# A recurrent block on one core: order of the decayed scores and of the 2:4 selection, and a first round with halves of products between the levels

## The chip, the cores and the metric

The kernel runs on one core of one Trainium2 chip. The metric is the device time of one execution in microseconds (us). TensorE is called PE here, VectorE DVE, ScalarE ACT, GpSimd POOL and SyncE SP. "L1275" is line 1275 of the kernel before.

## What is computed

Two blocks follow one another on 2048 tokens of 256 channels (two sequences of 1024). Each is a recurrent mixer, gated by a feed-forward branch, and added to its input.

```python
xn = layernorm(x)
s  = L0_attn(xn)      # five token-shift mixes, r/k/v/g projections, decayed outer-product recurrence
                      # (4 heads of 64), norm per head, times silu gate, output projection
g  = silu(L0_ffn(xn)) # h = silu(x@w_gate) * (x@w_up), 1024 wide;
                      # of each 4 neighbours the 2 largest |h| are kept (2:4); h @ w_down
x  = x + s * g
xn = layernorm(x)
s  = L1_attn(xn)      # state space: 8 heads, chunks of 32, scores C B^T times exp(cs_i - cs_j)
g  = silu(L1_ffn(xn)) # gated feed-forward, 1024 wide, not sparse
x  = x + s * g
```

## The kernel before

The tokens are cut into 8 tiles of 256. The kernel runs nine rounds. Round 1 does the first block of tile 0 alone. Each of the seven rounds of the loop does the first block of tile n (called `a`) and the second block of tile n-1 (called `b`), interleaved by hand. The last round does the second block of tile 7 alone. `one(a, b)` is written once for each engine and holds the order of the steps by hand for three cases: `a and b`, `a` alone (the first round), `b` alone (the last round). Every engine works through its list strictly in order, so a step that waits holds all that stands behind it on its engine.

PSUM has eight banks. Each product has a bank and a turn in it. `FILLS` says which for the loop, `FIRST_FILLS` for the first round. PE may open a bank for a product when the previous product of that bank has been freed by its reader (`open_bank`); the readers wait until it is filled (`wait_filled`).

Steps that matter here, with the lines of their instructions:

- The feed-forward branch of block one makes its hidden units in four pairs: `p0` to `p3`, each with a gate product (`p3g`) and an up product (`p3u`), eight 128x256 matmuls each (`project_p`, matmuls at L1275). ACT makes the tanh (`ffn_tanh`, L500), DVE two products (`hidden_p`, L799 and L803), ACT the absolute values (`ffn_abs`, L507). DVE compares the four neighbours (`compare`, L913), counts (`sparse_count`, L924 to L931) and sets the smaller ones to zero (`sparse_select(0)` for units of p0 and p1, `sparse_select(1)` for p2 and p3, L941). PE multiplies by the down weights (`down_0`, in the first round `down_part`, L1311) after both selections.
- The recurrence of block one runs through seven levels. PE makes the products of a level (`level`, L1364, the last at L1403), DVE multiplies k and r by decays and takes the products (`level_step`, three instructions, L868, L869, L877), and PE may start the next level then. `own_products` (L1384, banks `D0` and `D1`) makes the diagonal, which `own_keys` (L897) takes. After the last level come `last_update` (L868, L869), `keys_turned` (L1596), `chunk_states` (L1610), `states_0` (L992), `outputs` (L1420 to L1431), `centred` (L1006 to L1014), `variances`, the root on POOL, `out_normed` (L1025), `out_turned` (L1324), `out_gated` (L1035) and `out_0` (L1275).
- The state-space part of block two: POOL masks the sums, ACT takes sixteen exponentials (`L_exps(0)` and `L_exps(1)`, eight of 128x128 each, L546), PE makes the scores in four banks (`sc0`, `sc2` by `scores(0)`; `sc1`, `sc3` by `scores(1)`; L1459), and DVE multiplies them (`decayed_scores`, L1096). `sc0` and `sc1` need `L_exps(0)`, `sc2` and `sc3` need `L_exps(1)`. Then `states_1` (L1101, L1104) on DVE; `within` (L1474) on PE waits for all four, and `across` (L1485) for `states_1`. DVE gates the result (`gated_1`, L1114), which frees the banks `ys0` and `ys1` that the products `n1g` and `n1u` of the second feed-forward branch open next.

Of the kernel before, what the change touches and what calls it, by code (L numbers as in the profile page):

```python
# [20 lines left out]
ALU = mybir.AluOpType  # L21
# [54 lines left out]
               ["mix_k", "L1", "kv", "yT"],  # L76
               ["mix_r", "r", "D0", "Y0", "s0"],
               ["a", "mix_v", "v", "D1", "Y1"],
               ["p0g", "w0", "p2g", "g"], ["p0u", "w1", "p2u", "F0"], ["p1g", "mix_g0", "p3g"], ["p1u", "mix_g1", "p3u"]]
FIRST = {n: (b, i + 1) for b, names in enumerate(FIRST_FILLS) for i, n in enumerate(names)}  # L80
# [32 lines left out]
def build_block(nc, A):  # L113
    with ExitStack() as ctx:
# [96 lines left out]
        lev_pair = psum[:, BANK["L0"]:BANK["L0"] + 2, :]  # L211
        own_pair = psum[:, BANK["D0"]:BANK["D0"] + 2, :]

# [277 lines left out]
        def _(act):  # L491
# [44 lines left out]
            def one(a, b):  # L536
# [112 lines left out]
                if a and b:  # L649
# [28 lines left out]
                    end_exp()  # L678
                    L_exps(0)
                    L_exps(1)  # L680
                    ffn_tanh(a, "p3", th[1], th_ready, "p1")
                    copy(a, y[:, :, :], "Y0", NQ)
# [11 lines left out]
                elif a:  # L694
# [12 lines left out]
                    ffn_tanh(a, "p3", th[1], th_ready, "p1")  # L707
                    ffn_abs(a, 2)
                    others()
                    copy(a, k0n[:, :, :], "k0T", NQ)  # L710
                    ffn_abs(a, 3)
                    gate_tanh()
                    copy(a, y[:, :, :], "Y0", NQ)
# [36 lines left out]
        def _(dve):  # L750
# [139 lines left out]
            def own_keys(t):  # L890

                dve.wait_ge(lev_ready, t.count(6, 1))
                dve.sem_inc(passed, 1)
                for e in range(2):
                    wait_filled(dve, t, f"D{e}")
                    dve.sem_inc(passed, 1)
                    free(d.copy_predicated(own[:, e, :, :].rearrange("p g x -> p (g x)"), same[:, 256 * e:256 * e + 256],  # L897
                                           own_pair[:, e, 0:256]), t, f"D{e}")

# [58 lines left out]
            def one(a, b):  # L958
# [131 lines left out]

                def decayed_scores(part):
                    for n in (part, 2 + part):
                        dve.wait_ge(L_exp, b.count(NQ, n // 2 + 1))
                        wait_filled(dve, b, f"sc{n}")
                        w = flat(cs_row)[:, n * 512:(n + 1) * 512]
                        free(d.tensor_tensor(w, w, ps(b, f"sc{n}")[:, :], ALU.mult), b, f"sc{n}")  # L1096

# [30 lines left out]
                if a and b:  # L1128
# [37 lines left out]
                    B_decayed()  # L1166
                    sparse_select(0)
                    decayed_scores(0)
                    hidden_p(a, 3)
                    decayed_scores(1)  # L1170
                    states_1()
                    compare(1)
                    sparse_count()
                    gated_1()
                    sparse_select(1)
# [14 lines left out]
                elif a:  # L1190
# [18 lines left out]
                    level_step(a, 1)  # L1209
                    sparse_sums()  # L1210
                    sparse_rest()
                    level_step(a, 2)
                    mix_g_scaled(a)
                    mix_add(a, "g")
                    level_step(a, 3)
                    hidden_p(a, 2)
                    level_step(a, 4)
                    level_step(a, 5)
                    last_update(a)
                    hidden_p(a, 3)  # L1220
                    sparse_select(0)
                    compare(1)
                    states_0()
                    sparse_count()
                    sparse_select(1)
                    centred()
                    gate_0()
                    variances()
                    out_normed()
                    next_normed()  # L1230
                    out_gated()
# [4 lines left out]
                else:  # L1236
# [7 lines left out]
                    B_decayed()  # L1244
                    decayed_scores(0)
                    decayed_scores(1)
                    hidden_n(b, 2)
# [10 lines left out]
        def _(pe):  # L1258
# [34 lines left out]
            def project_p(t, n, suffix):  # L1293
                hidden_pair(t, f"p{n}{suffix}", {"g": "f_gate", "u": "f_up"}[suffix], n, lambda h: xnT[:, h, 1:T + 1])

            def ffn_p(t, n):
                project_p(t, n, "g")
                project_p(t, n, "u")
# [10 lines left out]
            def down_part(t, q, first, end):  # L1309
                for m in range(first, end):  # L1310
                    ins = t_.matmul(ps(t, "F0")[:, q * C:(q + 1) * C], hid[:, m, q * P:(q + 1) * P],  # L1311
                                    W["f_down"][:, m * C:(m + 1) * C], start=(m == 0), stop=(m == 7))
                return ins
# [61 lines left out]
            def own_products(t):  # L1375

                open_bank(t, "D0")
                open_bank(t, "D1")
                pe.sem_inc(passed, 1)
                ins = [None] * 2  # L1380
                for g in range(CH * NQ):
                    for e, hf in ((0, 0), (1, 1), (0, 1), (1, 0)):
                        r, n = slice(64 * e, 64 * e + 64), g * P + 64 * hf
                        ins[e] = t_.matmul(own_pair[64 * hf:64 * hf + 64, e, g * 64:(g + 1) * 64], flat(kT)[r, n:n + 64],  # L1384
                                           flat(rU)[r, n:n + 64], start=True, stop=True)
                for e in range(2):
                    close_bank(ins[e], t, f"D{e}")
# [107 lines left out]
            def one(a, b):  # L1495
# [84 lines left out]
                def gate_in():  # L1580
                    pe.wait_ge(mix_ready, a.count(5, 5))
                    proj(a, "g")

                def first_levels():
                    wait_freed(pe, a, "k")
                    wait_freed(pe, a, "r")
                    wait_freed(pe, a, "v")
                    own_products(a)
# [173 lines left out]
                elif a:  # L1762
# [13 lines left out]
                    values()  # L1776
                    first_levels()
                    gate_mix()
                    level(a, 1)
                    project_p(a, 2, "g")  # L1780
                    level(a, 2)
                    project_p(a, 2, "u")
                    level(a, 3)
                    project_p(a, 3, "g")
                    level(a, 4)
                    project_p(a, 3, "u")
                    level(a, 5)
                    level_last(a)
                    keys_turned()
                    chunk_states()  # L1790
                    gate_in()
                    outputs()
                    pe.wait_ge(loads["down0"], 16)
                    pe.wait_ge(sparse_ready, a.count(2, 2))
                    open_bank(a, "F0")
                    down_part(a, 0, 0, 8)
                    down_part(a, 1, 0, 6)
                    out_turned()
                    close_bank(down_part(a, 1, 6, 8), a, "F0")
                    next_turned()  # L1800
                    out_0()
# [98 lines left out]
```

## Time and profile before

| | us |
|---|---|
| median of 3 runs | 766.62 |
| lowest, highest | 766.07, 769.03 |
| the profiled execution, device time | 767.01 |
| span of its trace | 765.3 |
| mean granted clock of PE over the span | 0.990 of full speed |

The span runs from the first to the last instruction. 1.7 us of the device time lie around it. Round 1 takes the span's first 76.7 us, each loop round 91.0 to 92.0 us, the last round the rest from about 716.9 us. In the rows below, a bracket such as [0.51 <-issue] says how long the engine had been idle just before the row, and what ended that.

### The profile page before, as it was taken

How to read it: one execution, taken by the hardware profiler on the slowest of the kernel's cores; microseconds unless marked ns; L12 is line 12 of the kernel's file. 1: busy time of each engine (PE TensorE's matmuls, PEld its weight loads, DVE VectorE, ACT ScalarE, POOL GpSimd, SP SyncE). 2: the span in 40 equal slices, each digit the busy share in tenths (PEclk: the TensorE clock that was granted, in tenths of full speed). 3: DMA queues.
4: the chain of work that ended last, by engine and by line, in shares of the span. 5: the costliest groups of instructions: out<-in, count | busy, mean ns of one | idle time of the engine just before them, and what ended most of it. 6: DMA issues, size and time to landing. Idle time of an engine off the chain costs nothing.

```text
span 765.3 us, 18468 instructions
## 1 busy us (share of the span) xinstructions
PE 735.6 (96%) x7316; PEld 602.7 (79%) x7316; DVE 506.1 (66%) x1177; ACT 325.8 (43%) x659; POOL 76.1 (10%) x85
## 2 busy tenths in 40 slices
PE   4888999999999999999999999999999999999997
PEld 3666678877888788887888878888778878888686
DVE  3877679737797367945678467874679737795143
ACT  1312565126642366214752057512664236631570
POOL 6201011001011011000110001100011101100020
PEclk9879999999999999999999999999999999999999
DMA  8800320015000150002400032000500015000220
GB/s 291 318 1 15 116 39 3 1 30 153 2 3 1 44 139 2 3 2 71 112 2 2 3 121 60 3 1 30 147 8 3 0 44 140 2 3 1 96 57 15
DMA packets 33938, 39.77 MB, mean 52 GB/s; under 512 B 20352, under 2 KB 27968, under 8 KB 32192
## 3 DMA queue, kind: packets, MB, share of 16 engines
q1 hardware_dynamic: 33856, 38.49, 16.8%
q8 instruction: 75, 1.23, 0.7%
q14 instruction: 7, 0.06, 0.0%
HBM read 32.12 MB, written 6.36 MB: 50 GB/s over the span
## 4 chain that ended last, share of the span: by engine, by line
PE 93%; DVE 4%; issue 1%; ACT 1%; DMA 0%; POOL 0%; DVEq 0%; SPq 0%; ACTq 0%; POOLq 0%
PE psum L1275 72%; PE psum L1364 4%; PE psum L1474 2%; PE psum L1459 2%; PE psum L1324 1%; PE psum L1335 1%; PE psum L1485 1%; PE psum L1683 1%; PE psum L1512 1%; PE psum L1610 1%; PE psum L1384 1%; PE psum L1556 1%; PE psum L1420 1%; PE psum L1403 1%; PE psum L1427 1%
## 5 line engine op out<-in xcount | busy, mean ns | idle before, releaser
L520 ACT ACTIVATE BC<-psum 64x256 f32<-64x256 f32 x128 | 81.2, 634 | 3.5 <-PE psum L1275 1.8
L1275 PE MATMUL psum<-xnT,sb_f_gate 128*128 128x256 f32 x256 | 66.6, 404 | 1.8 <-issue 1.0
L1275 PE MATMUL psum<-xnT,sb_f_up 128*128 128x256 f32 x256 | 62.3, 385 | 0.0
L1275 PE MATMUL psum<-xn1T,sb_n_gate 128*128 128x256 f32 x256 | 61.4, 383 | 0.0
L1275 PE MATMUL psum<-xn1T,sb_n_up 128*128 128x256 f32 x256 | 60.5, 379 | 0.0
L1275 PEld LDWEIGHTS psum<-xnT,sb_f_gate 128*128 128x128 f32 x256 | 48.7, 198 | 11.6 <-issue 2.9
L1275 PEld LDWEIGHTS psum<-xn1T,sb_n_up 128*128 128x128 f32 x256 | 48.6, 190 | 6.6
L1275 PEld LDWEIGHTS psum<-xn1T,sb_n_gate 128*128 128x128 f32 x256 | 47.3, 190 | 6.5
L1275 PEld LDWEIGHTS psum<-xnT,sb_f_up 128*128 128x128 f32 x256 | 47.1, 189 | 6.6 <-issue 0.2
L868 DVE TENSOR_TENSOR kT<-kT,dec 128x256 f32<-128x256 f32 x56 | 25.2, 450 | 39.3 <-PE psum L1364 31.8
L1275 PE MATMUL psum<-sb_n_down,hidB 128*128 128x256 f32 x224 | 49.5, 379 | 0.0
L1275 PE MATMUL psum<-sb_f_down,hid 128*128 128x256 f32 x224 | 49.5, 379 | 0.0
L1119 DVE SCALAR_TENSOR_TENSOR thFB<-thFB,psum 128x512 f32<-128x512 f32 x8 | 5.5, 688 | 66.5 <-ACT thFB L647 66.5
L1275 PEld LDWEIGHTS psum<-sb_n_down,hidB 128*128 128x128 f32 x224 | 42.6, 190 | 5.8
L1275 PEld LDWEIGHTS psum<-sb_f_down,hid 128*128 128x128 f32 x224 | 42.6, 190 | 5.8
L500 ACT ACTIVATE thB<-psum 128x512 f32<-128x512 f32 x32 | 18.9, 592 | 66.3 <-PE psum L1275 66.3
L472 POOL TENSOR_SCALAR_AFFINE_SELECT cs_row<-cs_row 128x2048 f32<-128x2048 f32 x8 | 16.0, 2004 | 265.3 <-DMA cs_half<-cs_dram 265.3
L500 ACT ACTIVATE th<-psum 128x512 f32<-128x512 f32 x32 | 18.9, 592 | 54.4 <-PE psum L1275 54.4
L1364 PEld LDWEIGHTS psum<-rT,kT 64*64 64x64 f32 x1536 | 27.7, 137 | 15.1 <-issue 15.1
L647 ACT ACTIVATE thFB<-psum 128x512 f32<-128x512 f32 x8 | 4.8, 598 | 80.1 <-PE psum L1275 80.1
L546 ACT ACTIVATE cs_row<-cs_row,cs_col 128x128 f32<-128x128 f32 x128 | 38.2, 387 | 0.0
L1364 PE MATMUL psum<-rT,kT 64*64 64x32 f32 x1536 | 32.6, 223 | 1.6 <-DVE own L877 1.6
(203 smaller groups left out, 1496.4 us busy)
## 6 DMA issues: line engine op xcount, KB each, us to landing
cs_row<-cs_dram SPq DMA_DIRECT2D x8, 1024.0 KB, 5.2
x_dram<-gate SPq DMA_DIRECT2D x8, 512.0 KB, 2.8
cs_half<-cs_dram SPq DMA_DIRECT2D x16, 256.0 KB, 6.3
hidB<-x_dram SPq DMA_DIRECT2D x8, 512.0 KB, 7.9
X<-in_x SPq DMA_DIRECT2D x9, 256.0 KB, 2.8
x<-in_x SPq DMA_DIRECT2D x8, 256.0 KB, 2.7
out_tokens<-thFB SPq DMA_DIRECT2D x8, 256.0 KB, 2.2
sb_w_rkvgo<-in_w_rkvgo SPq DMA_DIRECT2D x1, 1280.0 KB, 5.7
```

Source lines behind the costliest of these rows:

```text
L472: g.affine_select(out=cs_row[:, :, :], in_=cs_row[:, :, :], compare_op=ALU.is_ge, fill=NEG, base=0, pattern=[[0, NQ * SCH], [1, P]], chann ...
L500: a_.activation(buf[:, :], ps(t, name + "g")[:, :], ACT.Tanh, scale=0.5).then_inc(ready, 1)
L520: ins = a_.activation(cols[:, par, 2 * pair:2 * pair + 2, :], src[64 * par:64 * par + 64, :, s, :], ACT.Identity)
L546: ins = a_.activation(cs_row[:, n, :], cs_row[:, n, :], ACT.Exp, bias=cs_col[:, n:n + 1])
L868: k_ins = d.tensor_tensor(kk[:, :, 0, :], kk[:, :, 0, :], two[:, :, 1:2].to_broadcast([P, n, s]), ALU.mult)
L1275: ins = t_.matmul(ps(t, name)[first_row:first_row + rows, col:col + n], w, x, start=(k == 0), stop=(k == len(ws) - 1))
L1324: ins = t_.transpose(ps(t, name)[:, h * T + q * P:h * T + (q + 1) * P], src[:, q, h * P:(h + 1) * P], ident[:, :])
L1335: ins = t_.matmul(ps(t, "mix_" + f)[:, h * T:(h + 1) * T], W["w_mix2a"][r, h * P:(h + 1) * P], aT[r, :], start=True, stop=True)
L1364: ins = t_.matmul(lev_pair[64 * hf:64 * hf + 64, e, g * 32:(g + 1) * 32], flat(kT)[r, n:n + 64], q, start=True, stop=True)
L1384: ins[e] = t_.matmul(own_pair[64 * hf:64 * hf + 64, e, g * 64:(g + 1) * 64], flat(kT)[r, n:n + 64], flat(rU)[r, n:n + 64], start=True, sto ...
L1459: ins[s] = t_.matmul(ps(t, names[s])[:, i * P:(i + 1) * P], Bf[r, c * P:(c + 1) * P], Cf[r, c * P:(c + 1) * P], start=True, stop=True)
L1474: t_.matmul(y_out(t, s, c, par), Xrow[:, s, c, :], m[:, par, :], start=(c == 0), stop=(c == 0), skip_group_check=True)
```

## The change

For the seven loop rounds: on ACT, the tanh of `p3` moves from behind `L_exps(1)` to between `L_exps(0)` and `L_exps(1)`. On DVE the scores are multiplied as 0, (`hidden_p(3)`), 2, 1, 3 instead of 0, 2, (`hidden_p(3)`), 1, 3. `sparse_select(0)` moves from before the scores to behind `states_1`, and `gated_1` moves ahead of `sparse_count`.

For the first round: `D0`, `D1` get other banks (behind `w0` and `w1`) and `p3g`, `p3u` take their places behind `r` and `v`; `first_levels` no longer waits for `v`. `p2g` goes ahead of level 1. The products `p2u`, `p3g`, `p3u` and the gate `g` are cut into halves of four matmuls, and two halves stand between levels; the gate product thus comes before the last level instead of behind `chunk_states`. The down product is cut in four pieces, of which the first two need `sparse_select(0)` alone, and `next_turned` goes ahead of `out_turned`. DVE and ACT get a new order to match. The last round's order is the same in other words.

```diff
-               ["mix_r", "r", "D0", "Y0", "s0"],
-               ["a", "mix_v", "v", "D1", "Y1"],
-               ["p0g", "w0", "p2g", "g"], ["p0u", "w1", "p2u", "F0"], ["p1g", "mix_g0", "p3g"], ["p1u", "mix_g1", "p3u"]]
+               ["mix_r", "r", "p3g", "Y0", "s0"],
+               ["a", "mix_v", "v", "p3u", "Y1"],
+               ["p0g", "w0", "D0", "mix_g0", "g"], ["p0u", "w1", "D1", "mix_g1", "F0"], ["p1g", "p2g"], ["p1u", "p2u"]]
...
                     L_exps(0)
+                    ffn_tanh(a, "p3", th[1], th_ready, "p1")
                     L_exps(1)
-                    ffn_tanh(a, "p3", th[1], th_ready, "p1")
...
                     ffn_abs(a, 2)
+                    gate_tanh()
                     others()
+                    ffn_abs(a, 3)
                     copy(a, k0n[:, :, :], "k0T", NQ)
-                    ffn_abs(a, 3)
-                    gate_tanh()
...
                     B_decayed()
-                    sparse_select(0)
                     decayed_scores(0)
                     hidden_p(a, 3)
+                    decayed_scores(2)
                     decayed_scores(1)
+                    decayed_scores(3)
                     states_1()
+                    sparse_select(0)
                     compare(1)
+                    gated_1()
                     sparse_count()
-                    gated_1()
                     sparse_select(1)
...
                     level_step(a, 1)
-                    sparse_sums()
-                    sparse_rest()
-                    level_step(a, 2)
                     mix_g_scaled(a)
                     mix_add(a, "g")
+                    level_step(a, 2)
+                    sparse_count()
                     level_step(a, 3)
                     hidden_p(a, 2)
                     level_step(a, 4)
+                    sparse_select(0)
                     level_step(a, 5)
+                    hidden_p(a, 3)
                     last_update(a)
-                    hidden_p(a, 3)
-                    sparse_select(0)
-                    compare(1)
+                    next_normed()
+                    sparse_compare(a, 1, 0)
                     states_0()
+                    sparse_compare(a, 1, 1)
+                    sparse_compare(a, 1, 2)
                     sparse_count()
+                    centred()
                     sparse_select(1)
-                    centred()
+                    variances()
                     gate_0()
-                    variances()
                     out_normed()
-                    next_normed()
...
+            def half_p(t, n, suffix, i):
+
+                name, w = f"p{n}{suffix}", {"g": "f_gate", "u": "f_up"}[suffix]
+                if i == 0:
+                    open_bank(t, name)
+                for h in range(CH):
+                    c = h * HID + (2 * n + i) * P
+                    ins = t_.matmul(ps(t, name)[:, i * T:(i + 1) * T], W[w][:, c:c + P], xnT[:, h, 1:T + 1],
+                                    start=(h == 0), stop=(h == CH - 1))
+                if i == 1:
+                    close_bank(ins, t, name)
...
                     first_levels()
+                    project_p(a, 2, "g")
+                    level(a, 1)
                     gate_mix()
-                    level(a, 1)
-                    project_p(a, 2, "g")
+                    half_p(a, 2, "u", 0)
                     level(a, 2)
-                    project_p(a, 2, "u")
+                    half_p(a, 2, "u", 1)
+                    half_p(a, 3, "g", 0)
                     level(a, 3)
-                    project_p(a, 3, "g")
+                    half_p(a, 3, "g", 1)
+                    half_p(a, 3, "u", 0)
                     level(a, 4)
-                    project_p(a, 3, "u")
+                    half_p(a, 3, "u", 1)
+                    half_gate_in(0)
                     level(a, 5)
+                    half_gate_in(1)
                     level_last(a)
                     keys_turned()
                     chunk_states()
-                    gate_in()
+                    pe.wait_ge(loads["down0"], 16)
+                    pe.wait_ge(sparse_ready, a.count(2, 1))
+                    open_bank(a, "F0")
+                    down_part(a, 0, 0, 4)
                     outputs()
-                    pe.wait_ge(loads["down0"], 16)
+                    down_part(a, 1, 0, 4)
                     pe.wait_ge(sparse_ready, a.count(2, 2))
-                    open_bank(a, "F0")
-                    down_part(a, 0, 0, 8)
-                    down_part(a, 1, 0, 6)
+                    down_part(a, 0, 4, 8)
+                    next_turned()
+                    down_part(a, 1, 4, 6)
                     out_turned()
                     close_bank(down_part(a, 1, 6, 8), a, "F0")
-                    next_turned()
                     out_0()
```

## Rows read from the trace of the kernel before

**Rows 1.** The page: PE's granted clock in 40 slices of the span, in tenths.
```profile
PEclk9879999999999999999999999999999999999999
```

**Rows 2.** Busy time in stretches; columns: stretch and length, engines, clock, DMA, GB/s.
```profile
259.70:350.80 91.10, 90.55 (x916) 74.70 (x915) 62.06 (x146) 40.52 (x82) 7.36 (x5) 1.00 0.14 39
```

**Rows 3.** PE's waits between 80 and 716 us: total, times, longest.
```profile
PE psum L1474 <- issue: 3.6, 7, 0.5
```

**Rows 4.** Timeline of PE in a loop round: start, us, instruction, idle before.
```profile
303.90 1.89 PE L1275 MATMUL psum<-xnT,sb_f_up 128*128 128x256 f32 x8
...
309.91 2.11 PE L1474 MATMUL psum<-cs_row,hidB 128*64 128x64 f32 x64 [0.51 <-issue]
...
316.49 1.89 PE L1275 MATMUL psum<-xn1T,sb_n_gate 128*128 128x256 f32 x8
...
319.95 7.07 PE L1275 MATMUL psum<-sb_f_down,hid 128*128 128x256 f32 x32
```

**Rows 5.** Timeline of DVE in the same round.
```profile
304.20 1.42 DVE L941 SCALAR_TENSOR_TENSOR hid<-wins,hid 128x256 f32<-128x256 bf16 x4
...
308.54 1.28 DVE L1096 TENSOR_TENSOR cs_row<-cs_row,psum 128x512 f32<-128x512 f32 x2
...
309.99 1.87 DVE L1104 SCALAR_TENSOR_TENSOR S<-S,chunk_dec,psum 128x64 f32<-128x64 f32 x6
```

**Rows 6.** Timeline of ACT in the same round.
```profile
301.72 4.77 ACT L546 ACTIVATE cs_row<-cs_row,cs_col 128x128 f32<-128x128 f32 x16
306.40 0.57 ACT L500 ACTIVATE th<-psum 128x512 f32<-128x512 f32 x1
```

**Rows 7.** Timeline of PE in the first round.
```profile
31.05 0.69 PE L1384 MATMUL psum<-rU,kT 64*64 64x64 f32 x32 [1.32 <-ACT v L511]
...
33.89 1.08 PE L1364 MATMUL psum<-rT,kT 64*64 64x32 f32 x32 [1.06 <-DVE own L877]
...
36.97 2.72 PE L1275 MATMUL psum<-xnT,sb_f_gate 128*128 128x256 f32 x6 [0.85 <-issue]
...
42.39 0.67 PE L1364 MATMUL psum<-rT,kT 64*64 64x32 f32 x32
...
44.91 0.67 PE L1364 MATMUL psum<-rT,kT 64*64 64x32 f32 x32
...
49.43 0.68 PE L1403 MATMUL psum<-rT,kT 64*64 64x64 f32 x16 [1.32 <-DVE own L877]
...
53.56 3.78 PE L1275 MATMUL psum<-mixed_g,sb_w_rkvgo 128*128 128x256 f32 x8
57.27 0.69 PE L1420 MATMUL psum<-S,rT 64*64 64x64 f32 x32
...
69.05 1.99 PE L1275 MATMUL psum<-sb_w_rkvgo,mixed_w 128*128 128x256 f32 x8 [0.54 <-DVE mixed_w L1035]
```

**Rows 8.** Timeline of DVE in the first round.
```profile
29.39 1.89 DVE L913 TENSOR_TENSOR beats<-habs 128x768 bf16<-128x768 f32 x3
...
45.65 0.43 DVE L868 TENSOR_TENSOR kT<-kT,dec 128x256 f32<-128x256 f32 x1
...
46.33 0.42 DVE L877 COPY_PREDICATED own<-masks,psum 128x256 f32<-128x256 int8 x1
...
55.49 0.98 DVE L992 SCALAR_TENSOR_TENSOR S<-S,dec,psum 128x64 f32<-128x64 f32 x4
...
61.78 0.69 DVE L1014 TENSOR_TENSOR mixed_r<-mixed_k,gsum 128x512 f32<-128x512 f32 x1
62.50 0.69 DVE L981 SCALAR_TENSOR_TENSOR gT<-gT,psum 128x512 f32<-128x512 f32 x1
```

**Rows 9.** Stretches of the first round, columns as in rows 2.
```profile
33.40:40.20 6.80, 5.46 (x64) 4.03 (x64) 3.85 (x10) 0.48 (x1) 0.00 (x0) 0.50 0.08 30
...
47.10:50.40 3.30, 1.69 (x50) 1.14 (x49) 1.28 (x4) 0.18 (x1) 0.00 (x0) 1.00 0.02 5
50.40:57.30 6.90, 5.88 (x32) 4.21 (x32) 6.76 (x18) 1.58 (x4) 0.00 (x0) 0.51 0.00 0
```

More of the change, by code:

```diff
@@ L211, in build_block @@
         lev_pair = psum[:, BANK["L0"]:BANK["L0"] + 2, :]
-        own_pair = psum[:, BANK["D0"]:BANK["D0"] + 2, :]
         def by_half(t, name):
@@ L897, in own_keys @@
                     free(d.copy_predicated(own[:, e, :, :].rearrange("p g x -> p (g x)"), same[:, 256 * e:256 * e + 256],
-                                           own_pair[:, e, 0:256]), t, f"D{e}")
+                                           by_half(t, "D")[:, e, 0:256]), t, f"D{e}")
             def last_update(t):
@@ L1089, in B_decayed, with decayed_scores @@
                                                  [P, SCH - 1, SD]), ALU.mult), b, f"bt{s}")
[L1091 to L1096, printed above, removed]
+                def decayed_scores(n):
+                    dve.wait_ge(L_exp, b.count(NQ, n // 2 + 1))
+                    wait_filled(dve, b, f"sc{n}")
+                    w = flat(cs_row)[:, n * 512:(n + 1) * 512]
+                    free(d.tensor_tensor(w, w, ps(b, f"sc{n}")[:, :], ALU.mult), b, f"sc{n}")
                 def states_1():
@@ L1244, in one @@
                     B_decayed()
-                    decayed_scores(0)
-                    decayed_scores(1)
+                    for n in (0, 2, 1, 3):
+                        decayed_scores(n)
                     hidden_n(b, 2)
@@ L1311, in down_part @@
                     ins = t_.matmul(ps(t, "F0")[:, q * C:(q + 1) * C], hid[:, m, q * P:(q + 1) * P],
-                                    W["f_down"][:, m * C:(m + 1) * C], start=(m == 0), stop=(m == 7))
+                                    W["f_down"][:, m * C:(m + 1) * C], start=(m == 0 and q == 0), stop=(m == 7),
+                                    skip_group_check=True)
                 return ins
@@ L1383, in own_products @@
                         r, n = slice(64 * e, 64 * e + 64), g * P + 64 * hf
-                        ins[e] = t_.matmul(own_pair[64 * hf:64 * hf + 64, e, g * 64:(g + 1) * 64], flat(kT)[r, n:n + 64],
+                        ins[e] = t_.matmul(by_half(t, "D")[64 * hf:64 * hf + 64, e, g * 64:(g + 1) * 64], flat(kT)[r, n:n + 64],
                                            flat(rU)[r, n:n + 64], start=True, stop=True)
@@ L1582, in gate_in, with half_gate_in @@
                     proj(a, "g")
+                def half_gate_in(i):
+                    if i == 0:
+                        pe.wait_ge(mix_ready, a.count(5, 5))
+                        open_bank(a, "g")
+                    for h in range(CH):
+                        c = 3 * 2 * C + h * C + i * P
+                        ins = t_.matmul(ps(a, "g")[:, i * T:(i + 1) * T], W["w_rkvgo"][:, c:c + P], mixed["g"][:, h, :],
+                                        start=(h == 0), stop=(h == CH - 1))
+                    if i == 1:
+                        close_bank(ins, a, "g")
                 def first_levels():
@@ L1586, in first_levels @@
                     wait_freed(pe, a, "r")
-                    wait_freed(pe, a, "v")
                     own_products(a)
```

## The prediction

> **What bounds the kernel now.** I read PE's clock over the span first, because it shows at once which part is unlike the rest: it is full everywhere but in slices 2 to 4, which lie in the first round [rows 1]. Then the busy times by stretch: in a loop round PE works 90.55 of 91.10 us, so the loop is bound by PE and holds 0.55 us a round that a new order can win [rows 2]. The waits of PE over the seven loop rounds name it: one wait of 0.5 us in each, 3.6 us in all, ahead of `within`, L1474 [rows 3]. The page calls its end "issue", but the last score multiplied on DVE ends at 308.54 + 1.28 = 309.82 and `within` starts at 309.91 [rows 4, 5]: PE waits for `decayed_scores`. The first round is the other place. Its PE has a string of waits for DVE and ACT in the recurrence, and two stretches of some 6.8 us at half clock (1.2 GHz), 33.4 to 40.2 and 50.4 to 57.3 [rows 7, 9].
>
> **Loop rounds, scores.** The instructions are the same, only their order changes, so the sum is about when the four scores are done. Now `sparse_select(0)` takes 1.42 us from 304.20, and then sc0, sc2, two products of `hidden_p(3)` and sc1, sc3 follow until 309.82 [rows 5]. In the new order sc0 can start where the selection did, at 304.20, if `L_exps(0)` is done. Sixteen exponentials and the step to the next instruction take 306.40 - 301.72 = 4.68 us, so eight take 2.34, and the half ends at about 304.1 [rows 6]: it is done. The tanh of p3 (0.57, some 0.5 to the next instruction) then pushes `L_exps(1)` from about 306.5 to 304.1 + 0.5 + 2.34 + 0.1 = 307.0 [rows 6]. On DVE sc0 ends at 304.9, the first product of `hidden_p(3)` at 305.5; its second one waits for `p3u`, which PE has ready at 303.90 + 1.89 = 305.8 [rows 4], and ends at 306.5. Then sc2, sc1, sc3 run from 307.0, at 0.6 us from one to the next (two in 1.28 us [rows 5]) to 308.95. PE would be ready for `within` at 309.91 - 0.51 = 309.40 by the profile [rows 4]. So the scores come 0.4 us ahead of PE, and the wait goes whole: 0.51 to 0.6 us a round, **3.6 to 4.2 us in seven rounds; I take 3.8**. DVE waits 0.5 us more for `L_exps(1)` than it does now; that costs nothing as long as these 0.4 us are there.
>
> **Loop rounds, what is late next.** `states_1` starts 0.8 us earlier and `across` needs it: it ends at 309.99 + 1.87 = 311.86 now [rows 5], and at 311.1 then, before `within` ends (309.40 + 2.11 = 311.5 [rows 4]). `sparse_select(0)` now stands between `states_1` and `gated_1`, which frees `ys0` for `n1g`. From 311.1: selection 1.34, comparison 1.89 [rows 8], first half of the gating 0.7, so `ys0` is free at 315.0; `n1g` would open at 316.49 - 0.5 = 316.0 [rows 4]. Cover 1.0 us. Both selections are done some 0.5 us later than now, at about 318.3, and the down product wants them at 319.95 - 0.5 = 319.4 [rows 4]: cover 1.1. Both edits at nothing.
>
> **First round, levels.** `own_products` waits 1.32 us for the copy of `v` and starts at 31.05; without that wait PE is ready at 29.73, and r, copied before v, is there [rows 7]. DVE is in `compare(0)` until 29.39 + 1.89 = 31.28 [rows 8], so its first level step begins there. A step takes 46.33 + 0.42 - 45.65 = 1.10 us, and 0.3 more in this first one, where the take from PSUM is longer [rows 8]: level 1 of PE can start at 32.75 instead of 33.89 [rows 7], with `p2g` already done in the gap. From there: `gate_mix` now needs the banks of `D0` and `D1`, free when `own_keys` ends at 33.7; PE waits 0.35 us. Then gate mix, half of `p2u`, level 2 at 35.4. Later levels follow at 44.91 - 42.39 = 2.52 us (a level and two halves, as now a level and a whole product [rows 7]): 37.9, 40.4, 42.9. DVE has 1.0 us of step and 1.3 to 1.5 of other work between them (`mix_g`, count, `hidden_p(2)`, selection of 1.42 [rows 5]), so it just keeps up and the last step ends at 44.8. Last level 44.85 against 49.43 [rows 7]: **4.6 us earlier**, of which 3.0 are the first stretch at half clock and its 0.85 us of "issue".
>
> **First round, behind the levels.** `hidden_p(3)` stands ahead of `last_update` now (1.3 us on DVE), so k is ready at 46.4 and PE waits 1 us. Transposes 0.6, copy by ACT 0.7, `chunk_states` 0.6 at full clock: filled at 48.4. `states_0`, 0.98 us [rows 8], ends at 49.4, and `outputs` start at 49.5 against 57.27 [rows 7]. They can, because the gate product (57.27 - 53.56 = 3.7 us at half clock [rows 7]) has been done between the levels. That is **7.8 us earlier**. From `outputs` to `out_0` are 69.05 - 57.27 = 11.8 us now [rows 7], a chain over DVE and POOL; in it `sparse_select(1)`, 1.42, replaces `gate_0`, 0.69 [rows 8], behind the centring (now 61.78 + 0.69 = 62.47 [rows 8]): 0.7 longer. `out_0` comes at 61.9, **7.1 us earlier**. The rest of the round hangs on `out_0` as it does now.
>
> **What this opens.** PE then stands before its third piece of the down product from 51.8 (outputs 1.6, four matmuls 0.9 from 49.5) until the second selection, 54.7 + 1.4 = 56.1: 4.3 us with nothing to do, longer than any wait that it now has behind its start. Both falls of the clock came behind or in such stretches (1.69 us busy of 3.30 before the second [rows 9]). So I expect one fall here; then `out_turned` and what is before it run at half clock, 0.3 to 1 us on the chain; I take 0.6. The trace doesn't show what the 0.85 us of "issue" were [rows 7]; they can come back beside a wait (0) or on the path (0.85); I take 0.4. First round: 7.1 - 0.6 - 0.4 = **6.1 us**, between 3 and 7.8.
>
> The Trainium skill, "TensorE: Matmul & The Clock Gate", section "Why this matters for your kernels", asks for no long idle gaps between matmul bursts, because an idle stretch puts the clock back to half. The trace agrees: it fell twice where PE had been waiting [rows 9]. By that rule the new 4.3 us wait must cost the clock; were it free, the sum would be 0.6 us better.
>
> **Sum.** 3.8 + 6.1 = 9.9 us. 767.01 - 9.9 = 757.1 for an execution like the profiled one, whose time is 0.4 above the median of 766.62; I give **757.0**. A measurement of this kernel tells some 0.5%, 3.8 us, from no change.
>
> **Rivals.**
> - *Two falls of the clock in the first round, or a long one* (chance 0.2). The waits that stay between 44.4 and 47.8 (0.45, 1.05, 0.7 us, 2.2 of 3.4) are like the 1.61 idle of 3.30 before the second fall [rows 9]; for it speaks that small products stand there too, against it that half of the gate product does as well. Then `chunk_states` to `outputs` run at half clock: 0.5 + 0.9 + 1.0 = 2.4 us more, or `out_0` and the products after it do, 1.7 more. 759.5 to 761.
> - *The loop's wait stays in another form* (0.1). If `L_exps(1)` or the scores come 0.9 us later than I reckon, `within` waits as now. The first round alone then: 767.0 - 6.1 = 760.9.
> - *The first round gives little* (0.06): the levels become bound by DVE, whose work between them is only 0.1 us under PE's, and the new wait before the second selection eats the rest. 767.0 - 3.8 - 1 = 762.2.
> - *Slower* (0.03). `sparse_select(0)` behind `states_1` holds up `gated_1`, and so `n1g`, seven times. It has 1.0 us of cover; it would need 2.4 us of delay on DVE to lose 1.4 a round, 7 x 1.4 = 9.9, and so the whole gain; at 3 us of delay the time is 767.0 + 7 x 2.0 - 9.9 = 771. Nothing in the rows gives such a delay: the absolute values that the comparison needs are made while PE does `within`.
> - Forecast, 0.61.
>
> **How the numbers follow.** The forecast's own range is 755 to 759 (first round 5 to 7.8, loop 3.6 to 4.2). The best bounds give 767.0 - 7.8 - 4.2 = 755.0, and I go 1 us lower for unseen small waits in the loop that may go too. At the upper end the range takes in the first two rivals, to 761.5. Left out are 0.09 at the upper end and something on either side of the sums. Faster by over 0.5% (under 762.8) are the forecast and the first two rivals, and most of the third: 0.93. I take off a little for what I can't see: 0.91, within 0.05, slower 0.04.
>
> **What would show each step.** Right: no wait before L1474 in the loop, and seven rounds of 90.5 to 90.7 us; sc2, sc1, sc3 in one run on DVE; `out_0` at about 62 to 63 us; last level near 45 us, `outputs` near 49.5; full clock from 33 to 40 us; one wait of some 4 us before the third piece of the down product, and half clock behind it. Wrong: a wait before L1474 of over 0.2 us, a wait of PE for `ys0`, the last level later than 47 us, or `out_0` after 65 us.

## The result, and the profile after

| | before | changed |
|---|---|---|
| median of 6 runs each, us | 766.49 | 762.05 |
| lowest, highest | 765.42, 770.09 | 761.22, 763.89 |
| profiled execution, device time | 767.01 | 761.46 |
| span of its trace | 765.3 | 759.7 |
| mean granted clock | 0.990 | 0.996 |

The ratio is 0.9942 (95% interval 0.9918 to 0.9965): 4.4 us faster, where 9.9 were forecast and 754.0 to 761.5 was the range. The same kernel on another chip (`after_again` below) gave 0.9931 (0.9919 to 0.9944).

The loop did what was forecast. These are PE's waits between 70 and 716 us in the changed kernel, all of them (us in total, times, longest):

```profile
PE psum L1338 <- DVE habs L779: 1.6, 1, 1.6
PE psum L1515 <- ACT xn1T L510: 0.7, 1, 0.7
PE psum L1378 <- DVE own L876: 0.6, 1, 0.6
PE psum L1276 <- DVE prefix L1056: 0.6, 1, 0.6
PE psum L1542 <- ACT aT_dtT L558: 0.2, 1, 0.2
```

The seven waits of 0.5 us ahead of `within` [rows 3] are gone, and no line took their place in every round. A loop round by stretch (columns as in rows 2) has 0.12 us of PE idle instead of 0.55:

```profile
257.69:348.48 90.79, 90.67 (x916) 74.53 (x915) 62.14 (x146) 40.52 (x83) 7.53 (x5) 1.00 0.15 40
```

The first round did not. PE's timeline there, to be held against rows 7 (start, us, instruction, idle before):

```profile
27.95 1.89 PE L1276 MATMUL psum<-sb_w_rkvgo,mixed_v 128*128 128x256 f32 x8
29.77 0.69 PE L1398 MATMUL psum<-rU,kT 64*64 64x64 f32 x32
...
33.19 0.67 PE L1378 MATMUL psum<-rT,kT 64*64 64x32 f32 x32 [0.35 <-DVE own L876]
34.23 0.45 PE L1361 MATMUL psum<-aT_dtT,sb_mix2b 32*128 32x128 f32 x3 [0.37 <-DVE own L896]
35.55 0.59 PE L1361 MATMUL psum<-aT_dtT,sb_mix2b 32*128 32x128 f32 x5 [0.86 <-issue]
36.07 1.13 PE L1304 MATMUL psum<-xnT,sb_f_up 128*128 128x256 f32 x4
37.14 1.08 PE L1378 MATMUL psum<-rT,kT 64*64 64x32 f32 x32
...
41.22 0.67 PE L1378 MATMUL psum<-rT,kT 64*64 64x32 f32 x32
...
48.27 0.68 PE L1417 MATMUL psum<-rT,kT 64*64 64x64 f32 x16 [0.26 <-DVE own L876]
...
51.77 1.99 PE L1324 MATMUL psum<-sb_f_down,hid 128*128 128x256 f32 x8
53.69 0.69 PE L1434 MATMUL psum<-S,rT 64*64 64x64 f32 x32
...
60.28 3.11 PE L1324 MATMUL psum<-sb_f_down,hid 128*128 128x256 f32 x8 [3.04 <-DVE hid L940]
63.19 1.06 PE L1338 MATMUL psum<-ident,xn 128*128 128x128 f32 x4
64.04 1.22 PE L1324 MATMUL psum<-sb_f_down,hid 128*128 128x256 f32 x4
65.09 0.60 PE L1338 MATMUL psum<-ident,mixed_k 128*128 128x128 f32 x4
...
67.53 1.99 PE L1276 MATMUL psum<-sb_w_rkvgo,mixed_w 128*128 128x256 f32 x8 [0.97 <-DVE mixed_w L1034]
```

Level 1 came at 33.19 (forecast 32.75), level 3 at 41.22 (37.9), the last level at 48.27 (44.85), `outputs` at 53.69 (49.5), `out_0` at 67.53 (61.9). So the trace has 69.05 - 67.53 = 1.5 us from the first round, and the remaining 765.3 - 759.7 - 1.5 = 4.1 from the loop. From the first matmul of the X product (`sb_w_X`) in round two to that in the last round ("the loop's length" below) are 635.8 us before and 631.7 in the changed kernel, which is the same 4.1. PE's idle time in it fell from 5.4 to 2.0 us. The other 0.7 us are busy time of PE, and no run shows where they come from.

The first round's time, and where the clock falls in it, differ between executions of the same code. Below, the first round is therefore measured from the start of the values product to the start of `out_0` ("V to out_0"): 41.20 us before, 39.58 in the changed kernel.

### The profile page after: what moved, and what is told of

It is laid out like the page before. It is cut to its first block, busy times and chain, and to the rows that moved or that the text cites. A ratio compares the mean times of both kernels' runs of the same rounds, so it can differ in the third digit from the quotient of the medians.

```text
span 759.7 us, 18508 instructions
## 1 busy us (share of the span) xinstructions
PE 733.9 (97%) x7316; PEld 601.5 (79%) x7316; DVE 505.5 (67%) x1177; ACT 326.0 (43%) x659; POOL 76.6 (10%) x85
## 4 chain that ended last, share of the span: by engine, by line
PE 93%; DVE 4%; issue 1%; ACT 1%; DMA 0%; POOL 0%; DVEq 0%; SPq 0%; ACTq 0%; POOLq 0%
PE psum L1276 70%; PE psum L1378 4%; PE psum L1488 2%; PE psum L1473 2%; PE psum L1338 2%; PE psum L1349 1%; PE psum L1499 1%; PE psum L1707 1%; PE psum L1526 1%; PE psum L1304 1%; PE psum L1324 1%; PE psum L1361 1%; PE psum L1434 1%; PE psum L1634 1%; PE psum L1441 1%
## 5 line engine op out<-in xcount | busy, mean ns | idle before, releaser
L1276 PE MATMUL psum<-xnT,sb_f_gate 128*128 128x256 f32 x248 | 62.6, 396 | 1.0 <-ACT xnT L532 0.8
L1276 PE MATMUL psum<-xnT,sb_f_up 128*128 128x256 f32 x240 | 58.3, 385 | 0.0
L1276 PEld LDWEIGHTS psum<-xnT,sb_f_gate 128*128 128x128 f32 x248 | 46.2, 194 | 9.9 <-issue 1.7
L1276 PE MATMUL psum<-sb_n_down,hidB 128*128 128x256 f32 x224 | 49.5, 379 | 0.0
L1276 PE MATMUL psum<-sb_f_down,hid 128*128 128x256 f32 x224 | 49.5, 379 | 0.0
L1276 PEld LDWEIGHTS psum<-xnT,sb_f_up 128*128 128x128 f32 x240 | 44.2, 189 | 6.2 <-issue 0.2
L798 DVE SCALAR_TENSOR_TENSOR thB<-thB,psum 128x512 f32<-128x512 f32 x32 | 21.9, 685 | 18.5 <-ACT thB L499 18.2
```

Of the source, the lines that this page charges most:

```text
L798: free(d.scalar_tensor_tensor(out=buf[:, :], in0=buf[:, :], scalar=1.0, in1=ps(t, name + "g")[:, :], op0=ALU.add, op1=ALU.mult), t, name + ...
L1276: ins = t_.matmul(ps(t, name)[first_row:first_row + rows, col:col + n], w, x, start=(k == 0), stop=(k == len(ws) - 1))
```

## Experiments: which part of the change has the gain

**One part at a time.** `e1_loop_only` has the new orders of the loop and the first round of before; `e2_first_only` the reverse.

> The first round as in the kernel before, the loop rounds as in the changed one. Theory A (the loop gives what the sum of the prediction said, and the first round is where the forecast failed): 4.0 us less than the kernel before, about 762.5, no wait before the products within (L1474 of the kernel before), first 128x256 product of round two at 76.6 us. Theory B (the two parts depend on each other, because the loop takes over whatever the first round leaves): under 2 us or over 5.5 us less.

> The first round as in the changed kernel, the loop rounds as before. Theory A: 1.5 us less than the kernel before, with run-to-run differences of the order of 1 us where the clock of TensorE falls once more or once less; the wait of 0.5 us before within is there in all seven rounds. Theory B: over 2.5 us less, the rest of the 4.4 us.

Measured: `e1` 763.36 us, ratio 0.9947 (0.9930 to 0.9964), that is 4.1 us faster. `e2` 766.84 us, ratio 0.9994 (0.9978 to 1.0011): nothing that can be told from zero. Theory A holds for the loop; its 1.5 us for the first round do not show in the times. The trace of `e2` is that of its slowest execution (770.81 us), so it does not explain the median, but it shows how far the stretch V to out_0 can go. Here it is in `e2` (columns as in rows 2):

```profile
29.09:71.53 42.44, 35.05 (x437) 27.17 (x435) 30.73 (x78) 9.96 (x19) 2.98 (x2) 0.84 0.15 57
```

In the changed kernel, with the same code in this stretch:

```profile
27.95:67.53 39.58, 32.17 (x437) 25.07 (x435) 30.76 (x78) 9.96 (x19) 2.98 (x2) 0.91 0.19 74
```

In the kernel before:

```profile
27.85:69.05 41.20, 33.44 (x437) 26.18 (x436) 30.79 (x78) 9.97 (x19) 2.98 (x2) 0.83 0.16 66
```

The same instructions took 39.58 us at a mean clock of 0.91 and 42.44 at 0.84, and at that clock the new order is 1.2 us longer than the old one at 0.83.

**Which edit of the loop.** `e3_select_moved` moves only the selection, `e4_scores_order` only the scores and the tanh, both in the kernel before.

```diff
 # e3, loop rounds, VectorE
                     B_decayed()
-                    sparse_select(0)
                     decayed_scores(0)
                     decayed_scores(2)
                     hidden_p(a, 3)
                     decayed_scores(1)
                     decayed_scores(3)
                     states_1()
+                    sparse_select(0)
                     compare(1)
+                    gated_1()
                     sparse_count()
-                    gated_1()
```

```diff
 # e4, loop rounds, VectorE (and the tanh of p3 between the halves on ScalarE)
                     sparse_select(0)
                     decayed_scores(0)
-                    decayed_scores(2)
                     hidden_p(a, 3)
+                    decayed_scores(2)
                     decayed_scores(1)
                     decayed_scores(3)
```

> The kernel before with sparse_select(0) behind states_1 and gated_1 ahead of the count in the loop; the scores stay in the order 0, 2, hidden_p(3), 1, 3 and the tanh of p3 behind both halves of the exponentials. Theory S (the 1.42 us of the selection ahead of the scores are what TensorE waits for): 3.6 to 4 us less. Theory O (the order against the exponentials matters): VectorE comes to sc2 1.4 us earlier and waits there for L_exps(1), which ends at the same time as before, and hidden_p(3) still waits for its tanh behind it; the scores end at the same 309.8, and the time is that of the kernel before within 0.7 us.

> The kernel before with the scores in the order 0, hidden_p(3), 2, 1, 3 and the tanh of p3 between the two halves of the exponentials in the loop; sparse_select(0) stays ahead of the scores. Theory S: no gain, since the 1.42 us are still ahead. Theory O: sc0 at 305.5, hidden_p(3) until 307.5 without a wait, then three scores until 309.3, just ahead of TensorE at 309.4: the wait of 0.5 us becomes 0 to 0.1, and the time is 3 to 4 us less than before, nearly that of the whole loop edit.

Measured: `e3` 766.67 us, ratio 0.9994 (0.9978 to 1.0011); `e4` 764.61 us, ratio 0.9961 (0.9945 to 0.9978), 3.0 us faster. That is theory O. The loop's length says the same: 635.9 us in `e3`, 633.0 in `e4`. VectorE in `e3`, sc0 and then sc2:

```profile
303.50 0.69 DVE L1095 TENSOR_TENSOR cs_row<-cs_row,psum 128x512 f32<-128x512 f32 x1
305.75 0.69 DVE L1095 TENSOR_TENSOR cs_row<-cs_row,psum 128x512 f32<-128x512 f32 x1 [1.56 <-ACT cs_row L546]
```

The 1.42 us that the selection left free [rows 5] became a wait of 1.56 us for the second half of the exponentials, and PE waits ahead of `within` as before, by its list of waits:

```profile
PE psum L1475 <- issue: 3.5, 7, 0.5
```

In `e4` the last three scores run without a wait behind `hidden_p(3)`. DVE's row for them:

```profile
305.36 1.87 DVE L1095 TENSOR_TENSOR cs_row<-cs_row,psum 128x512 f32<-128x512 f32 x3
```

`within` on PE starts 0.1 us behind them, with no idle time noted in this round:

```profile
307.34 2.12 PE L1475 MATMUL psum<-cs_row,hidB 128*64 128x64 f32 x64
```

In one of the seven rounds of `e4`, `within` did wait, for 0.4 us; in the changed kernel and in `e1` it never did. So the order of the scores and the tanh together carry at least 3 of the loop's 4 us; the two were not tried one without the other. The move of the selection alone is worth nothing that shows. On top of the order it is worth at most the difference of `e1` and `e4` (4.1 to 3.0 us, whose intervals overlap).

## Experiments: where the first round loses

Each of the next three is the changed kernel with one edit in its first round; `after_again` is the changed kernel beside them.

> The changed kernel itself, on the same chip as the three others, so that they can be held against it. The time is 4.4 us under that of the kernel before, and the mean granted clock between 0.990 and 0.996, with 1.2 us more time for every 0.003 less.

Measured: 762.39 us, ratio 0.9931 (0.9919 to 0.9944); its clock was 0.995 or 0.996 in all six runs, V to out_0 39.66 us. Of the six runs of the first comparison, the three at 0.995 and 0.996 took 761.2 to 761.5 us, the two at 0.993 762.6 and 763.4, the one at 0.990 763.9. Between the means of these groups a step of 0.003 costs 0.9 to 1.6 us, where 1.2 was expected. It is a tendency and no more: the changed kernel took 762.0 to 762.9 us here, about 1 us more than in the first comparison at the same clock, and `e1` took 762.67 us at 0.990 and 763.6 at 0.998.

```diff
 # e5
-                    centred()
                     sparse_select(1)
+                    centred()
                     variances()
 # e6
+                    outputs()
                     pe.wait_ge(loads["down0"], 16)
                     pe.wait_ge(sparse_ready, a.count(2, 1))
                     open_bank(a, "F0")
                     down_part(a, 0, 0, 4)
-                    outputs()
 # e7, TensorE
                     level(a, 1)
-                    gate_mix()
                     half_p(a, 2, "u", 0)
                     level(a, 2)
+                    gate_mix()
                     half_p(a, 2, "u", 1)
 # e7, VectorE
                     level_step(a, 1)
-                    mix_g_scaled(a)
-                    mix_add(a, "g")
-                    level_step(a, 2)
                     sparse_count()
+                    level_step(a, 2)
+                    mix_g_scaled(a)
+                    mix_add(a, "g")
                     level_step(a, 3)
```

> The changed kernel with sparse_select(1) ahead of centred instead of behind it, in the first round alone. Theory W (TensorE stands 3 us before the third piece of the down product, falls to half clock and is then late for out_turned by 1.6 us): the selection ends near 56.8, the third piece starts at once behind the second, the clock does not fall at 61, out_turned starts as soon as the normed output is there (63.5), and out_0 at 66.0 instead of 67.5: 1.5 us less than the changed kernel, 760.5. Theory V (the chain over VectorE sets the end, the selection only changes its place in it): out_0 0.8 us later or the same, time of the changed kernel.

> The changed kernel with the first piece of the down product behind the outputs instead of ahead of them, in the first round alone. The piece was reckoned at 0.9 us in the prediction, and takes 1.9. Theory P (it stands on the path to the outputs): they start at 52.9, when states_0 ends, instead of 53.7, and all behind them moves 0.8 us forward: 0.8 us less than the changed kernel. Theory V (the outputs would wait for VectorE anyway): no difference.

> The changed kernel with gate_mix behind level 2, and its products on VectorE behind level step 2, in the first round alone. Theory M (gate_mix waits for own_keys, and with the 0.86 us of issue and what follows takes the clock down at 37): level 2 starts at about 35.6 instead of 37.1, level 3 at 38.1 to 38.6 instead of 41.2, full clock, outputs some 2.5 us earlier, time 2 to 3 us under that of the changed kernel. Theory I (the 0.86 us belong to the place in TensorE's instruction stream, some 107 matmuls behind the values product, whatever stands there): the stall comes inside the products p2u, level 2 starts at 36.2 to 36.5, and the clock may fall still; gain 0.5 to 1 us.

| | median, us | ratio to before (95%) | V to outputs | V to out_0 | clock in it |
|---|---|---|---|---|---|
| changed, beside them | 762.39 | 0.9931 (0.9919 to 0.9944) | 25.81 | 39.66 | 0.91 |
| e5, selection first | 761.38 | 0.9920 (0.9901 to 0.9939) | 25.78 | 38.53 | 0.92 |
| e6, outputs first | 761.16 | 0.9926 (0.9905 to 0.9946) | 25.05 | 37.89 | 0.91 |
| e7, gate mix later | 760.22 | 0.9905 (0.9890 to 0.9920) | 23.35 | 37.13 | 0.95 |

**e7** is the clearest: 2.2 us under the changed kernel beside it, with intervals that only touch. PE's timeline of `e7`:

```profile
33.61 0.67 PE L1378 MATMUL psum<-rT,kT 64*64 64x32 f32 x32 [0.35 <-DVE own L876]
34.21 1.13 PE L1304 MATMUL psum<-xnT,sb_f_up 128*128 128x256 f32 x4
36.08 0.67 PE L1378 MATMUL psum<-rT,kT 64*64 64x32 f32 x32 [0.74 <-DVE own L876]
36.68 0.71 PE L1361 MATMUL psum<-aT_dtT,sb_mix2b 32*128 32x128 f32 x8
37.33 1.13 PE L1304 MATMUL psum<-xnT,sb_f_up 128*128 128x256 f32 x4
38.30 1.03 PE L1304 MATMUL psum<-xnT,sb_f_gate 128*128 128x256 f32 x4
39.25 0.67 PE L1378 MATMUL psum<-rT,kT 64*64 64x32 f32 x32
```

From level 1 to level 3 are 5.6 us here and 41.22 - 33.19 = 8.0 in the changed kernel. Gone are the wait for `own_keys` (0.37), the 0.86 of "issue", and the half clock that followed them. A wait of 0.74 for VectorE ahead of level 2 is new. This is theory M. The stall that theory I expected inside `p2u` isn't there. A second trace of this code (`e10`, below) agrees up to level 3, in 5.95 us.

**e5** removed the 3.04 us wait, as theory W says, and `out_turned` starts as soon as `out_normed` ends. V to out_0 fell by 1.1 us, not 1.5: PE now waits inside the fourth piece of the down product for the normed output, and the clock falls behind that wait:

```profile
63.65 0.89 PE L1338 MATMUL psum<-ident,mixed_k 128*128 128x128 f32 x4 [3.44 <-DVE mixed_k L1024]
64.33 1.91 PE L1324 MATMUL psum<-sb_f_down,hid 128*128 128x256 f32 x4
66.38 2.46 PE L1276 MATMUL psum<-sb_w_rkvgo,mixed_w 128*128 128x256 f32 x8
```

Its time is 1.0 us under the changed kernel's, with overlapping intervals. The trace shows the mechanism of theory W, but 1.1 us is less than the same code varies by in this stretch, so the size of the gain is not shown.

**e6** brought `outputs` 0.8 us forward, as theory P expected; the times (1.2 us less) overlap here too. V to out_0 fell by 1.8 us, which is more than the step: the clock fell at 53.7, behind waits of 1.18 us at most; the down product ran at half clock until 57.1 beside the work of VectorE; and the wait ahead of its third piece shrank from 3.04 to 0.22 us, with full clock behind it.

**All three, and a repeat.**

> The changed kernel with all three edits of the first round at once: gate_mix behind level 2, the first piece of the down product behind the outputs, sparse_select(1) ahead of centred. Theory Q (the three losses of the first round lie one behind the other on one path): outputs 3.1 us earlier than in the changed kernel, counted from the start of the values product, out_0 4 to 4.5 us earlier, time 758.5 to 759.5, which is 0.990 of the kernel before or less. Theory R (they share one cover, since each also decides where the clock falls): no better than gate_mix later alone, which measured 0.9905.

> The kernel e7_gate_mix_later once more, beside the one with all three edits on the same chip. Theory R (the three losses share one cover, gate_mix later has nearly all of the gain): 0.9905 of the kernel before, and within 0.7 us of the kernel with all three.

> The kernel e8_all_three once more, on the same chip. Theory Q (the other two edits add the 1.1 and the 0.7 us that their traces showed, less what they share): 1.2 to 1.8 us less than gate_mix later alone. Theory R: no more than 0.7 us less.

Measured: all three 758.43 us, ratio 0.9898 (0.9882 to 0.9915). That fits theory Q by the time, but not by the trace: V to out_0 is 36.49 us, 3.2 us less than in the changed kernel, where 4 to 4.5 were expected. On one chip side by side, gate mix later (`e10`) took 759.83 us, ratio 0.9899 (0.9881 to 0.9918), and all three (`e11`) 759.76, ratio 0.9893 (0.9874 to 0.9911): 0.1 us apart in the median, as theory R says. With six runs each, spread over 2 us, this speaks against the 1.2 us of theory Q but does not exclude it.

The traces do not show the shared cover of theory R either. V to out_0 is 39.17 us in `e10` and 36.18 in `e11`, 3.0 us less. But in `e11` the values product starts 1.3 us later, and the loop's length is 633.1 us against 631.6 for the same code. So these two executions end 0.2 us apart. In all traces with the loop's new orders, that length lies between 631.5 and 633.1 us; no run shows why.

`e10` also corrects what one trace of `e7` seemed to say. In `e7` the clock fell once in the first round. In `e10`, the same code, it fell twice, at 49.6 and at 59.9, and V to `outputs` was 25.20 us where `e7` has 23.35. The first piece of the down product and the start of `outputs` in `e10`:

```profile
49.30 3.50 PE L1324 MATMUL psum<-sb_f_down,hid 128*128 128x256 f32 x8
52.73 0.81 PE L1434 MATMUL psum<-S,rT 64*64 64x64 f32 x32
```

The 2.1 to 2.4 us up to level 3 and the time of the kernel repeat; V to out_0 (37.13 and 39.17) does not. Either kernel is faster than every other version measured, 7.4 to 8.1 us under the kernel before and, by the ratios, some 3 us under the changed one.

**The wait that ends with "issue".**

```diff
 # e9, first round of the kernel before, TensorE
                     first_levels()
-                    gate_mix()
                     level(a, 1)
                     project_p(a, 2, "g")
+                    gate_mix()
                     level(a, 2)
```

> The kernel before with one move in TensorE's list of the first round: gate_mix behind the product p2g instead of ahead of level 1. The wait of 0.85 us that ends with issue stood behind the second of eight matmuls of p2g, the 106th behind the values product; in the changed kernel behind the third of gate_mix, the 107th. Theory I (it belongs to a place in the instruction stream): it now stands behind the first two or three matmuls of gate_mix, which are the 105th to 107th. Theory J (it belongs to an operand or to a wait of the product): it stays behind the second matmul of p2g, or goes. Time within 1 us of the kernel before either way.

Measured: 767.64 us, ratio 1.0016 (1.0001 to 1.0031), at the edge of a loss. The wait is at neither place:

```profile
32.67 0.65 PE L1364 MATMUL psum<-rT,kT 64*64 64x32 f32 x32
35.02 0.67 PE L1364 MATMUL psum<-rT,kT 64*64 64x32 f32 x32 [1.70 <-DVE own L877]
35.62 3.22 PE L1275 MATMUL psum<-xnT,sb_f_gate 128*128 128x256 f32 x8
38.77 1.12 PE L1347 MATMUL psum<-aT_dtT,sb_mix2b 32*128 32x128 f32 x8
```

With the gate mix out of it, the wait for VectorE ahead of level 1 grew from 1.06 [rows 7] to 1.70 us, and "issue" is gone. But this cannot be put down to the move. `e1`, `e3` and `e4` have the first round of before as it was, and the same wait of 1.06 us ahead of level 1, and "issue" is in none of them. In `e1`, all eight matmuls of `p2g` run in one row:

```profile
36.14 1.08 PE L1365 MATMUL psum<-rT,kT 64*64 64x32 f32 x32 [1.06 <-DVE own L877]
37.16 3.78 PE L1276 MATMUL psum<-xnT,sb_f_gate 128*128 128x256 f32 x8
```

So in the old order the stall shows in one trace of four, and `e9` decides nothing between theories I and J. In the changed kernel's first levels it shows in all five traces (0.86 to 0.93 us, in `e2`, `e5` and `e6` too), and with gate mix later in none of four. What it is, and why the order matters there, stays open.

## Why the prediction was wrong

- **The bound and the loop's sum: right.** 3.8 us forecast, 4.1 in the trace and 4.1 in `e1`; of the 4.1, 3.4 are idle time of PE, which is what the sum was about, so that the closeness is in part luck. The steps hold by their numbers. In the changed kernel, VectorE (start, us):

```profile
301.86 0.69 DVE L1094 TENSOR_TENSOR cs_row<-cs_row,psum 128x512 f32<-128x512 f32 x1
302.47 0.68 DVE L798 SCALAR_TENSOR_TENSOR th<-th,psum 128x512 f32<-128x512 f32 x1
303.42 0.69 DVE L802 TENSOR_TENSOR hid<-th,psum 128x512 f32<-128x512 f32 x1 [0.27 <-PE psum L1276]
304.74 1.88 DVE L1094 TENSOR_TENSOR cs_row<-cs_row,psum 128x512 f32<-128x512 f32 x3 [0.63 <-ACT cs_row L545]
```

  The scores end at 306.62, and `within` starts at 306.93 with no idle time: a lead of 0.3 us against 0.4 reckoned. `ys0` and the down product were never waited for, as the step "what is late next" said.
- **The step that failed, "First round, levels": 3.3 us.** The forecast has full clock from 33 to 40 us and level 3 at 37.9; it came at 41.2. The wait for `own_keys` is as reckoned (0.35, measured 0.37). But the "issue" stall came whole and on the path, inside the gate mix (0.86, the upper end of my bounds; I took 0.4, in another step). Behind waits of 0.35, 0.37 and 0.86 us between 32.8 and 35.6, the clock fell at 37.1, a cost that this step had put at nothing. `e7` takes the last two waits and the half clock out and gets 2.4 us back up to level 3, `e10` 2.1, and each kernel time fell by about as much. What share of that is the stall's and what the clock's was not separated.
- **Step "behind the levels": a term mis-sized.** I priced a piece of the down product, of four products, at 0.9 us, half the eight matmuls of p2u. It is 1.99: four products of the code are eight matmuls in the trace (the half of p2u that I took it from is two products, and shows as four). In front of `outputs` that fits the 0.84 us by which the distance from `chunk_states` to `outputs` exceeds the forecast; `e6` gets 0.8 back.
- **"What this opens": the place right, the effect too small.** The wait came, and the clock fell behind it. It was 3.04 us and not 4.3, since the second piece is longer, too; besides, the prediction's own terms give 49.5 + 1.6 + 0.9 = 52.0 and a wait of 4.1, not 51.8 and 4.3. But I let PE be ready for `out_turned` when the normed output is, within 1 us. Between the selection and `out_turned` stand the third piece, `next_turned` and half of the fourth piece, 60.28 to 65.09, while `out_normed` had ended at 63.47: 1.6 us late. By the rule of the Trainium skill that the prediction quotes ("TensorE: Matmul & The Clock Gate", section "Why this matters for your kernels"), this wait would cost the clock. The trace agrees: full clock until 61.0, then half until 64.4. The other falls in these two kernels are not cases of a long gap: the longest wait close before one is 0.86 us at 37.1 in the changed kernel, and 1.32 us at 33.4 and at 50.4 in the kernel before.

The busy times by stretch of the changed kernel show both falls (clock in the third column from the right):

```profile
33.20:37.10 3.90, 2.66 (x44) 1.92 (x44) 2.88 (x8) 0.27 (x1) 0.00 (x0) 1.00 0.28 107
37.10:40.60 3.50, 3.50 (x39) 2.95 (x39) 3.15 (x9) 0.00 (x0) 0.00 (x0) 0.51 0.00 0
57.30:60.30 3.00, 0.02 (x1) 0.02 (x1) 2.93 (x8) 0.63 (x1) 0.00 (x0) 1.00 0.00 0
61.10:64.60 3.50, 3.50 (x12) 2.88 (x11) 1.34 (x2) 0.00 (x0) 1.64 (x1) 0.53 0.00 0
```

Together: level 3 was 3.3 us late, `outputs` 4.2, `out_0` 5.6. Of these 5.6 the forecast had booked 1.0 (0.6 for the clock, 0.4 for "issue"), which leaves the 4.6 us between the 6.1 forecast and the 1.5 measured. Both signs that the prediction named for a wrong first round came: a last level after 47 us and `out_0` after 65. One reading of the rows was off as well: of the 40 slices, only 2 and 3 lie under 0.9, not 2 to 4 [rows 1].

- **Under all of these: the before.** I took 41.20 us for what the old first round costs and 7.1 us as certain to come off. It was one draw. The four traces with the old first round give, for V to out_0, 41.20 us and 40.56 (`e1`) at a mean clock of 0.83, 39.65 at 0.87 (`e3`) and 38.91 at 0.96 (`e4`). The last of them:

```profile
28.92:67.83 38.91, 29.69 (x437) 23.95 (x435) 30.69 (x78) 10.08 (x19) 2.98 (x2) 0.96 0.17 68
```

  The three with the new first round give 39.6 and 39.7 at 0.91, and 42.4 at 0.84. So up to 2.3 us of what the forecast booked on the edit (41.20 - 38.91) come and go with the execution at one and the same order, together with its clock. Against that spread the new first round is worth nothing that `e2` could show.
- **Rivals.** "Two falls of the clock" is what happened, at 37 and 61. The one at 61 is the fall that the forecast has itself; the other came not at the place I named (44 to 48), and I priced it at 2.4 us where the first round lost 4.6 of 6.1. "The first round gives little" is the nearest by its time (762.2, measured 762.05), and had a chance of 0.06. That is luck in the number. Of its mechanism, the levels were not bound by VectorE, which itself waited 0.91 us for the gate mix of PE and 1.12 us for level 3; the new wait ahead of the second selection did cost, with the half clock behind it. The range ended 0.55 us under the result.

## What to carry to other kernels

Ask of a freed engine what it runs into next: moving 1.42 us of selection out of the way gave nothing, and ordering the scores by when their exponentials are ready, with the tanh between the halves, gave 3 of 4 us. When pieces are cut finer to fill gaps, check for each what stands behind it on the in-order engine: moving one small piece (0.65 us of gate mix) from a place where it waited for a late reader gave 2.2 us. Before a saving in a stretch with a varying clock is booked, compare that stretch in several executions of the same code: one trace of `e7` showed one fall of the clock, a second of the same code two.

## What the runs showed that I had not expected

- The stretch V to out_0 varies by 2.9 us for identical code (39.58 and 42.44), with a mean granted clock in it of 0.91 and 0.84. In `e2` the clock fell three times in this stretch, at 38, 52 and 62. With gate mix later the two traces are 2.0 us apart.
- The start of the values product, ahead of every edit, lies between 27.53 (`e10`) and 30.10 us (`e1`) after the span's start.
- Where the clock falls moves with the order and with the execution: in `e5` it stands behind a later wait (3.44 us), in `e6` at 53.7 us, in `e8` and `e11` once and for 7 us, from 49 to 56. Side by side the kernel with all three edits is no faster than gate mix later alone, although V to out_0 is 3.0 us shorter in its trace.
- The loop is not a fixed length either: 631.5 to 633.1 us in nine traces with its new orders, and 635.8 to 637.2 in three with the old ones (before, `e2`, `e9`).
